# A graph network kernel: the node work at the ends of its passes, streamed, moved ahead or narrowed

## What is computed

```python
def conv(h, W, b):                       # three of these, relu after the first two
    m = concatenate([h[dst], h[src], edge_attr], axis=1) @ W + b
    return segment_sum(m, dst, n_nodes)
x = layernorm(x + conv(relu(conv(relu(conv(x, W1, b1)), W2, b2)), W3, b3))
# two PNA layers:
m = concatenate([x[dst], x[src], edge_attr @ We.T + be]) @ Wp.T + bp
agg = [mean, min, max, std, sum] of m over dst
out = concatenate([x, agg, agg*amp, agg*att]) @ Wo.T + bo ; out = out @ Wl.T + bl
x   = relu(batchnorm(out) * g + b)       # statistics over the nodes
x = layernorm(x + pna(pna(x)))
```

## Time and profile before

| what | us |
|---|---|
| median of 3 runs | 8141.34 (8137.03 to 8143.66) |
| the profiled execution | 8128.06, span 8126.3 |
| first conv pass, its 25 node quads | 1375.55 to 1508.06 |
| second conv pass, end of the block | about 2604 |
| third conv pass, end of the block | about 3688 |
| middle norm | 3688.9 to 3754.8 |
| batch norm | 5893.4 to 5933.8 |

### The profile page before, as it was taken

How to read it: one execution, slowest core, us unless ns; L and a number is a source line. 1 busy time by engine, 2 the same in 40 slices (tenths; PEclk the granted TensorE clock), 3 DMA queues, 4 the chain that set the end, 5 groups by cost and what they waited for, 6 DMA issues and landing times. The chain is left out here.

```text
span 8126.3 us, 167963 instructions
## 1 busy us (share of the span) xinstructions
PE 6793.0 (84%) x53896; PEld 5553.6 (68%) x53897; DVE 4444.9 (55%) x5962; ACT 2307.4 (28%) x3815; POOL 5634.3 (69%) x5891
## 2 busy tenths in 40 slices
PE   5999999889997898895788788887868788888886
PEld 4777777788886888885666666665656566666664
DVE  7888886322222222225666666666566666566566
ACT  4878876100000000002222222222232222222223
POOL 4666664477775777774777777777557777777774
PEclk9999998688887888897999998888989889898897
DMA  5666666477776777773222222222232222222222
GB/s 183 238 236 244 236 239 205 167 269 278 284 277 227 287 282 269 272 262 113 72 67 68 72 67 72 68 70 69 59 84 70 70 67 71 69 71 67 72 72 70
DMA packets 415308, 1226.32 MB, mean 151 GB/s; under 512 B 120178, under 2 KB 219852, under 8 KB 366574
## 3 DMA queue, kind: packets, MB, share of 16 engines
q1 hardware_dynamic: 214343, 743.70, 25.6%
q0 software_dynamic: 187712, 233.42, 13.3%
q10 hardware_dynamic: 13160, 248.08, 7.6%
HBM read 943.22 MB, written 281.51 MB: 151 GB/s over the span
## 5 line engine op out<-in xcount | busy, mean ns | idle before, releaser
L1947 POOL DMA_INDIRECT data<-q_rows,idx x3328 | 3160.2, 950 | 1123.5 <-issue 1001.3
L922 POOL DMA_INDIRECT data<-h_parts,idx x2508 | 2427.6, 968 | 1202.3 <-issue 1019.6
L1054 PE MATMUL p_z<-hs,adj 128*128 128x192 bf16 x22442 | 2115.6, 252 | 61.5 <-issue 61.5
L1054 PEld LDWEIGHTS p_z<-hs,adj 128*128 128x128 bf16 x22442 | 1934.6, 100 | 313.4 <-issue 105.3
L2079 ACT COPY back<-p_back 128x1024 f32<-128x1024 f32 x418 | 423.3, 1013 | 2375.2 <-PE p_back L1967 2375.2
L2149 DVE TENSOR_TENSOR_SCAN run<-reset,run,p_turn 128x1024 f32<-128x1024 bf16 x416 | 974.5, 2342 | 147.2 <-PE p_turn L2014 142.8
L1169 ACT CAST adj<-p_count 128x1012 bf16<-128x1012 f32 x836 | 920.0, 1101 | 213.3 <-PE p_count L1040 190.0
L575 DVE TENSOR_TENSOR hot<-p_ramp,ends 128x2048 f32<-128x2048 f32 x416 | 950.0, 2284 | 0.5 <-issue 0.4
L1973 PE MATMUL part<-hot,t 128*128 128x128 f32 x6688 | 910.3, 295 | 44.9 <-issue 44.9
L1973 PEld LDWEIGHTS part<-hot,t 128*128 128x128 f32 x6688 | 879.1, 212 | 45.5 <-issue 45.5
L1978 PE MATMUL part<-hot,back 128*128 128x128 f32 x6688 | 815.1, 275 | 0.0
(11 more groups left out here) (324 smaller groups left out, 6381.9 us busy)
## 6 DMA issues: line engine op xcount, KB each, us to landing
adj<-counted SPq DMA_DIRECT2D x304, 1568.0 KB
counted<-adj ACTq DMA_DIRECT2D x76, 3136.0 KB
reset<-flags SPq DMA_DIRECT2D x208, 512.0 KB
data<-q_rows,idx POOLq DMA_INDIRECT x3328
data<-h_parts,idx POOLq DMA_INDIRECT x2508
feat<-in_ea_blocks SPq DMA_DIRECT2D x208, 128.0 KB
ea<-in_ea_cols SPq DMA_DIRECT2D x154, 88.0 KB
rden<-node_rows SPq DMA_DIRECT2D x50, 256.0 KB
```

Of the source, the lines that this page charges most:

```text
L922: pool.indirect_dma_start(out=data[:, p % HELD, j, 0:PARTS], out_offset=None, in_=table[:, :], in_offset=bass.IndirectOffsetOnAxis(ap=idx[ ...
L1054: mm = pe.matmul(p_z[:, 0:PARTS], adj[:, (q + LAG) % 2, hi, :], hs[:, hi, :], start=(hi == 0), stop=(hi == BLOCKS - 1))
L1947: pool.indirect_dma_start(out=data[:, r, j, :], out_offset=None, in_=q_rows[:, :], in_offset=bass.IndirectOffsetOnAxis(ap=idx[:, r, j:j + ...
```

## The change

1. First conv pass: the node quads are written as a software pipeline over the engines (`pipeline` with lags), in transposed form: counts spread over 64 rows by one product with a wider `wsum`, h turned and scaled by them, sums and own products added in one PSUM bank, relu, transposed back, split into bf16 parts. Two quads are in flight.
2. Second and third pass: the finished quads of a turn are worked on before the last gathered group of the next turn (in the program order of TensorE, ScalarE and VectorE), and the last quad of all (24) is taken out of the table of quads and done last with two blocks of four (`END`).
3. Third pass: `normalised` adds x, takes off the mean and stores the centered rows, with the sum of squares of each row kept in `var`. SyncE loads x quad by quad (`load_x`).
4. Middle norm (`first_rows`): loads the centered rows and `var`, one root, one reciprocal, scales on VectorE, four buffers deep; only the source weights are loaded in front, the other shared loads go by GpSimd's queue; q is kept whole and stored in five pieces.
5. Batch norm: 12 steps of eight blocks and one of two, buffers four deep, rows and q kept whole, seven stores each.
6. PNA passes: the last quad is done after the loop on 256 columns, without its own statistics step.

```diff
+END = -(-N // P) - (QUADS - 1) * QUAD
-                v.memset(bounds[:, n, turns + 1:turns + 2], QUADS)
+                v.memset(bounds[:, n, turns + 1:turns + 2], QUADS - 1)
...
+            def load_x(n):
+                if not isinstance(n, int) or n:
+                    sp.wait_ge(s_x, n * 16)
+                    gate(sp)
+                sp.dma_start(x_in[:, bass.ds((n & 1) * QUAD, QUAD), :], by_partition(x_rows)[:, bass.ds(n * QUAD, QUAD), :])\
+                  .then_inc(s_x, 16)
...
+            def node_enter(n, i, half):
+                reused(pe, s_n_counts, n)
+                gate(pe)
+                pe.matmul(node_counts[i], wsum[:, D:], acc[0:KC, at_quad(n)], start=True, stop=True).then_inc(s_n_counted, 1)
+                reused(pe, s_n_scaled, n)
+                gate(pe)
+                for b in range(QUAD):
+                    for m in range(3):
+                        at = hs[:, bass.ds(n * QUAD + b, 1), m * D:(m + 1) * D].rearrange("p a f -> p (a f)")
+                        mm = pe.matmul(node_turned[i][:, b * P:(b + 1) * P], at, chip.identb[:, :], start=(m == 0),
+                                       stop=(m == 2))
+                mm.then_inc(s_n_turned, 1)
+                reused(pe, s_n_relu, n)
+                gate(pe)
+                pe.matmul(node_sums[i], wsum[:, 0:D], acc[0:KC, at_quad(n)], start=True, stop=False)
+            def node_own(n, i, half):
+                pe.wait_ge(s_n_scaled, n + 1)
+                gate(pe)
+                pe.matmul(node_sums[i], wa[:, :], scaled_t[:, i, :], start=False, stop=True).then_inc(s_n_own, 1)
+            def node_back(n, i, half):
...
+                for b in range(QUAD):
+                    mm = pe.transpose(node_rows[i][:, b, :], relu_t[:, i, b * P:(b + 1) * P], chip.ident[0:D, 0:D])
+                mm.then_inc(s_n_back, 1)
...
+                            pe.wait_ge(s_zs, k * NQ + NQ)
+                            pe.wait_ge(s_dense_added, k * NQ + NQ)
+                            pe.wait_ge(s_added, k * H + (nth[pos] + 1))
+                        if pos == POS_P[-1] and not first:
+                            finished_quads(pe, quads_of(pe, chip.quads, k - 1), convolve, banks_read)
...
                             turn(k, pos)
-                            finished_quads(pe, finished, convolve, banks_read)
...
-                with pe.Fori(0, QUADS) as n:
-                    convolve(n)
+                pipeline(pe, (0, node_enter), (1, node_own), (2, node_back))
             else:
                 finished_quads(pe, quads_of(pe, chip.quads, KT - 1), convolve)
+                convolve(QUADS - 1, END)
...
+                    pipeline(act, (1, node_relu), (0, node_count), (3, node_mid), (2, node_high))
+                    pipeline(v, (0, node_scale), (2, node_rest), (3, node_low))
...
+            def normalised(n, blocks):
+                v.tensor_tensor(conv[:, 0:blocks, :], conv[:, 0:blocks, :], part_s[:, 0:blocks, 0:D], ALU.add).then_inc(s_conv, 1)
+                v.wait_ge(s_x, n * 16 + 16)
+                v.tensor_tensor(to, conv[:, 0:blocks, :], x_in[:, bass.ds((n & 1) * QUAD, blocks), :], ALU.add).then_inc(s_step, 1)
+                v.tensor_reduce(means[:, 0, 0:blocks], to, AX_X, ALU.add).then_inc(s_step, 1)
+                v.tensor_scalar(means[:, 1, 0:blocks], means[:, 0, 0:blocks], 1.0 / D, None, ALU.mult).then_inc(s_step, 1)
+                v.tensor_tensor(to, to, means[:, 1, 0:blocks].unsqueeze(2).broadcast_to([P, blocks, D]), ALU.subtract)\
+                v.tensor_tensor(squares[:, 0:blocks, :], to, to, ALU.mult).then_inc(s_step, 1)
+                v.tensor_reduce(var[:, bass.ds(n * QUAD, blocks)], squares[:, 0:blocks, :], AX_X, ALU.add).then_inc(s_h, 1)
...
+def first_rows(chip, x_rows, var_rows, w, q_rows, shared):
...
+            sp.dma_start(var[:, 0, :], var_rows).then_inc(s_var, 16)
             for n in range(PIECES):
+                sp.dma_start(b[:, piece(n), :], by_partition(x_rows)[:, piece(n), :]).then_inc(s_b[n], 16)
+                if n == 0:
+                    sp.dma_start(*shared[2]).then_inc(s_source, 16)
...
+            for tile, rows in rest:
+                pool.dma_start(tile, rows).then_inc(s_shared, 16)
...
+            scale(0)
+            for c in range(NCH):
+                if c % CHUNKS == 0 and c // CHUNKS + 1 < PIECES:
+                    scale(c // CHUNKS + 1)
+                v.wait_ge(s_q, c + 1)
+                v.tensor_copy(q[:, c * B:(c + 1) * B, :], p_q[:, c % DEEP, 0:B * D].rearrange("p (b f) -> p b f", b=B))\
+                 .then_inc(s_stage, 1)
...
             nodes(pe, TURNS, of_nodes)
+            of_nodes(QUADS - 1, END * P)
...
+    STEPS = [(n * 2 * B, B) for n in range(BLOCKS // (2 * B))]
+    STORES = list(range(1, len(STEPS) - 1, 2)) + [len(STEPS) - 1]
...
+            for n, (at, blocks) in enumerate(STEPS):
+                if n >= DEEP:
+                    act.wait_ge(s_q, n - DEEP + 1)
+                stats.normalise_blocks(nc, xt[:, n % DEEP, :], at, blocks).then_inc(s_x, 1)
```

More of the change, by code:

```diff
@@ L1082, in convolve @@
                 gate(pe)
[L1083 to L1084 removed]
+                for b in range(blocks):
+                    mm = pe.matmul(p_part[:, b * (D + 1):(b + 1) * (D + 1)], sums[:, b * P:(b + 1) * P], wsum[:, 0:D + 1],
                                    start=True, stop=True)
@@ L1089, in convolve @@
                 gate(pe)
-                for b in range(QUAD):
-                    mm = pe.matmul(p_own[:, b * D:(b + 1) * D], h_t[:, b * P:(b + 1) * P], wa[:, :], start=True, stop=True)
+                for b in range(blocks):
+                    mm = pe.matmul(p_node[:, b * D:(b + 1) * D], h_t[:, b * P:(b + 1) * P], wa[:, :], start=True, stop=True)
                 mm.then_inc(s_own, 1)
@@ L1107, in _ @@
                             by_window(k, pos, POS_P.index(pos))
-                        if pos == POS_P[-1] and not first:
-                            finished = quads_of(pe, chip.quads, k - 1)
                         if not first:
@@ L1240, in _ @@
                         p = POS_P.index(pos)
+                        if pos == POS_P[-1] and not first:
+                            nodes(k)
                         act.wait_ge(s_row[p], k * (16 * GC) + 16 * GC)
@@ L1244, in _ @@
                           .then_inc(s_idx[p], 1)
-                        if pos == POS_P[-1] and not first:
-                            nodes(k)
                     elif first:
@@ L1555, in _ @@
                             sum_z(k, q)
+                        if pos == POS_P[-1]:
+                            nodes(finished)
                         sum_places(k, pos)
@@ L1571, in _ @@
                 finish_dense(KT, 0, KT * H + (1 + BEFORE), dense_begin_of(KT, 0))
-            nodes(None if first else quads_of(v, chip.quads, KT - 1))
+            nodes(None if first else quads_of(v, chip.quads, KT - 1), True)
 def pipeline(eng, *stages):
@@ L1733, in _ @@
-            sp.wait_ge(s_shared, 16 * len(shared))
+                sp.wait_ge(s_norm, n + 1)
+                sp.dma_start(by_partition(x_rows)[:, piece(n), :], b[:, piece(n), :]).then_inc(s_out, 16)
+                sp.wait_ge(s_stage, (n + 1) * CHUNKS)
+                sp.dma_start(by_partition(q_rows)[:, piece(n), :], q[:, piece(n), :]).then_inc(s_out, 16)
+            sp.wait_ge(s_out, 32 * PIECES)
         @block.gpsimd
         def _(pool):
-            for n in range(PIECES):
-                norm.scale(pool, n)
+            rest = shared[:2] + shared[3:]
@@ L2238, in normalise, with normalise_blocks @@
         return ins
+    def normalise_blocks(self, nc, to, block, blocks):
+        for h in range(2):
+            at = slice((block + h * blocks) * P, (block + (h + 1) * blocks) * P)
+            ins = nc.scalar.activation(to[h * D:(h + 1) * D, 0:blocks * P], self.chip.acc2[0:D, 0, at], ACT.Relu,
+                                       bias=self.shift[:, 0:1], scale=self.by[:, 0:1])
+        return ins
 def four_blocks(rows):
```

417 lines of the change are left out of this document (233 added, 184 removed).

## The result

| | before | changed |
|---|---|---|
| median of the runs, us | 8140.91 (4 runs, 8137.03 to 8143.66) | 8053.31 (4 runs, 8045.10 to 8055.63) |
| profiled execution, us | 8128.06, span 8126.3 | 8055.63, span 8053.6 |
| ratio, 95% interval | 1 | 0.9892 (0.9881 to 0.9904) |

The kernel became 87.6 us faster, where 79 were forecast, and 8053 lies in the range of 8036 to 8098. The sum came this close in part by luck, as errors of opposite sign cancel. To see them I cut both spans at GpSimd's gathers (its indirect loads of source rows): what the change touches lies between the last gather of a pass and the first of the next.

What follows compares the result with a forecast made beforehand. Edge passes were taken as bound by gathers or TensorE, with short stages between, which alone change. Terms -15 -11 +1 -30 -10 -14 = -79 us take 8128.06 to 8049, plus 13.3 gives 8062 us; range 8036 to 8098, leaving out (c).

Steps and rivals of the forecast that it cites:

- Part 1: First conv pass, streamed node quads: 4.45 us a quad, 117.5 us against 132.5, -15 us (-23 to +3).
- Rival (c): First pass's streamed quads: TensorE stays at the lower clock, 7.9 us a quad, kernel slower at 8158 us; chance 0.08.
- Rival (a): First pass's stream is bound by issue and waits, period 5.2 us, +18, so 8080 us; chance 0.13.
- Part 2: Second pass's end: two quads move into the wait for the last gather, -11 us (-14 to -6).
- Part 3: Third pass's end: same move, but added VectorE work makes two quads overrun the arrival, +1 us (-3 to +7).
- Part 4: Middle norm: less work and input, TensorE starts at +6.7 instead of +25.7, 35.5 us against 65.9, -30 (-34 to -20).
- rival (b): Middle norm is bound by transfers, giving -20 us instead of -30, so 8072 us; chance 0.06.
- Part 5: Batch norm: fewer, wider ScalarE activations, 21.3 us against 31, -10 us (-12 to -4).
- Part 6: Last PNA block at half width, both passes: -8 us in the first layer, -6 in the second, -14 (-17 to -8).
- The 13.3 us between profile and median: Whole kernel: profiled execution lies 13.3 us below the runs' median of 8141.34; distance carried from 8049 to the forecast 8062.

Runs made afterwards that it cites:

- the version with one product: Changed kernel with each quad's sums and counts from one product, second PNA layer's weights loaded in batch norm: ratio 0.9884; with addition before scaling, 0.9869.

## Why the prediction was right or wrong

**Part 1 (-15, measured -28.5): right mechanism, terms too large.** The three wide products were priced right (2.9 for 3.0). The turnings were mis-sized: the earlier trace rows shows 1.42 us at the lower and 1.74 at the head of the stage, I took both as issue, not as the clock, and let it run ahead only in part, at 1.0. In the stream they cost 0.67 at the upper level and 1.28 at the lower, and 0.64 more when doubled. The turning back is 0.39 for 0.45. 24 x (4.45 - 3.92) = 13 us, nearly all of the miss. The bound of -23 was too narrow, since its 4.1 us took the turnings at 0.7 but every other term at full price. The step from the parts' bounds to the range was wrong as well: added as independent, as the prediction says, they give about -90 to -55 us and not -99 to -58, and the stretches' -91.8 lie just outside.

**Rival (c): it did not come for the wide products, but a stream can fall.** At 64 columns the stream falls to 0.52, a quad takes 10.06 us and the kernel is slower than before. At 128 and 512 columns it stays up, so (c)'s own price, 7.9 us for a quad of wide products at the lower level, was never paid. The Trainium skill, "TensorE: Matmul & The Clock Gate", Part 1, has activity release the throttle and gives the lower level as that of an idle engine. By that rule the 64-column stream, busy 150 of 150 us, would not have fallen; the trace does not agree, and it was right to keep the rival against the rule.

**Rival (a)** fell: there is no wait in the quad. It did hold for the version with one product, until the addition was moved.

**Part 2 (-11, measured -13.8): right, and the excess is chance.** The two quads took 9.4 us on TensorE (about 10 forecast), and the tail took 11.0 for 11.5. The gain varies: the stretch was 35.6 to 41.6 us in eight profiles with the quads ahead (the pausing chip left out), against 47.7 to 49.3 in three of the kernel's old form. What varies is how late TensorE ends the last dense group, 1.5 to 6.8 us after the last gather. From 2.1 us on, TensorE has no wait left before the gathered group, and the overrun takes from the gain. The forecast took over the 4.1 us of the profile before; the changed kernel's profile had 1.9. On average the gain is 48.5 - 37.6 = 10.9 us, the forecast.

**Part 3 (+1, measured -2.4).** A quad's rows take 4.2 us on VectorE, not 4.8, and VectorE is through with the two quads ahead 15.9 us after the last gather, where 18.6 was forecast; nearly all of the difference is there. Put back, the quads cost 3.7.

**Part 4 (-30, measured -30.1): right sum, wrong reason in part.** TensorE starts at 6.4 (forecast 6.7) but its chunks take 0.7 instead of 0.85 us and it is done by 26.5; then the stage waits for transfers. The end, which I had put at TensorE plus one store, is set by 12.3 MB of transfers: 8.9 us lie behind the last issue, and 0.74 MB less make it 2.4 to 2.8 us shorter. That is rival (b)'s mechanism at the forecast's length: (b) stood at -20 because it took writes at about 250 GB/s, and no run shows that rate for them; with loads and stores in flight the stage moved 388 to 424 GB/s from 3660 to 3680.

**Part 5 (-10, measured -9.3): right sum.** An activation of 512 columns takes 0.81 us (0.84 forecast). The width alone gives 5.9 us, where the working had 31 to 21.3 from it; the rest came with the buffers and stores.

**Part 6 (-14, measured -9.8 in the two profiles).** Against full width on the changed kernel it is -7.4 and -7.5. The term that failed is the second block's -6: I read it off the one row in which no product fell to the lower level, halved it, and in the changed kernel the block had the first six of its nine products at the lower one. The halving itself was right: in the run with 64 columns all nine narrow products of the first block stayed at the upper level, and it took 10.9 us, 6.7 less than the 17.6. What was missing was a second profile of the kernel before.

**The 13.3 us between profile and median** were carried over unchanged, but they look like a matter of the chip and not of the kernel. The kernel before took 8134.8 to 8143.7 us on some chips and 8119.3 to 8135.4 on others; its profiled execution, 8128.06, lies in the second group and the median of 8141.34 in the first. The changed kernel's profile lay 2.3 us above its median. So the two profiles differ by 72.4 us and the medians by 87.6.

The five gathered stretches show the same. They took 7513.7 to 7519.5 us in three profiles of the kernel's old form and 7520.6 to 7538.8 in nine of the new, as a gather of a PNA pass took 0.948 to 0.954 us on average from one profile to another (the 0.956 us and the 6672 gathers of one expectation are wrong: there are 5836). A good part of this goes with the chip: the four profiles on the chip where the kernel before takes 8139 gave 7530.1 to 7538.1, and the changed kernel's own 7538.8 is like them, while on the two chips with 8127 the new form gave 7520.6 to 7530.3, against 7513.7 and 7517.8 for the old. Whether the change has a part in the rest (where its tensors lie, say) wasn't tried and stays open.

## What to carry to other kernels

Price an operation from a row in the middle of a train at the level at which it will run. Where a stage of narrow products stands at the lower level with an engine that is never idle, as here, try the same sums with wide moving operands early. After an engine is freed, look in the timeline for the in-order queue that reaches a finished input late; moving one instruction ahead of another was worth as much here as taking a product out. Cut a long span at the events that pace it, take two profiles before a block of 20 us is used as a term, and compare a profile with a median only if both come from one chip.

## What the runs showed of the hardware

- One stream of float32 products: at 512 and 128 columns the granted clock was 1.00 and 0.98, at 64 columns (with twice the weight loads) 0.52, with TensorE busy 150 of 150 us; with wide products and a fifth of the time idle, 0.89. Short trains are another matter: in the PNA blocks, behind a wait of 2.5 us, five products of 512 columns ran at the lower level.
- Twelve bf16 turnings of 128 columns, from their start to the next product's, took 1.28 us at the lower level and 0.67 at the upper behind wide products, but about 1.7 at the head of a quad that had waited, at the upper level too.
- Float32 products of 128 columns whose weights alternate started every 0.36 us; the four pieces of the counts, with one set of weights, took 0.92, which is 0.23 each.
- On one chip TensorE paused in the passes over edges, 1124.5 us in all in the dense bf16 products alone, with a mean granted clock of 0.745 over the span, while the streamed float32 quads ran at 1.00.
- The mean duration of an indirect gather on GpSimd moved between 0.948 and 0.954 us from one profile to another in the PNA passes, and the 1664 of such a pass took 2083.0 to 2094.2 us.
